# FFN tile by tile with keys as rows and squares turned through DRAM, in a fused cross-attention and FFN kernel

## The reference

```python
x = x + xattn(layernorm(x), ctx)      # 8 heads of 128; softmax of stretched scores over all 154 context rows
n = layernorm(x)
prev = n shifted down by one row within its batch (zeros first)
xr = mu_r * n + (1 - mu_r) * prev
xk = mu_k * n + (1 - mu_k) * prev
x = x + sigmoid(xr @ W_r.T) * (square(relu(xk @ W_k.T)) @ W_v.T)
```

## Time and profile before

| what | value |
|---|---|
| median of 3 runs | 744.74 us (743.87 to 744.83) |
| the profiled execution's own time | 744.54 us |
| its span in the trace | 742.7 us |
| PE busy | 736.4 us (99%) |
| DVE busy | 516.0 us (69%) |
| ACT busy | 426.8 us (57%) |
| POOL busy | 123.7 us (17%) |
| PE clock granted | full speed in all 40 slices |
| DMA | 106.52 MB, 143 GB/s |

### The profile page before, as it was taken

How to read it: one execution, slowest core, us unless ns; L and a number is a source line. 1 busy time by engine, 2 the same in 40 slices (tenths; PEclk the granted TensorE clock), 3 DMA queues, 4 the chain that set the end, 5 groups by cost and what they waited for, 6 DMA issues and landing times.

```text
span 742.7 us, 13556 instructions
## 1 busy us (share of the span) xinstructions
PE 736.4 (99%) x3948; PEld 643.0 (87%) x3948; DVE 516.0 (69%) x1085; ACT 426.8 (57%) x1204; POOL 123.7 (17%) x279
## 2 busy tenths in 40 slices
PE   9999999999999999999999999999999999999998
PEld 8957888888988888898888889888888988888887
DVE  3678987777667766666776766677666667766662
ACT  3568865575746556564655656465665646565332
POOL 1111111202121120212112021211202121120211
PEclk9999999999999999999999999999999999999999
DMA  9966643545444353545435354543535454343301
GB/s 330 252 152 172 202 136 115 148 147 177 140 146 147 117 164 87 176 142 167 129 109 159 93 175 144 163 126 115 167 84 175 143 167 128 109 156 93 112 28 43
DMA packets 87239, 106.52 MB, mean 143 GB/s; under 512 B 9999, under 2 KB 64169, under 8 KB 87211
## 3 DMA queue, kind: packets, MB, share of 16 engines
q1 hardware_dynamic: 87172, 106.15, 47.6%
q10 hardware_dynamic: 39, 0.04, 0.0%
HBM read 58.70 MB, written 47.45 MB: 143 GB/s over the span
## 4 chain that ended last, share of the span: by engine, by line
PE 90%; SPq 5%; DVE 1%; DMA 1%; ACT 1%; issue 1%; POOL 0%; POOLq 0%; DVEq 0%
PE ffn L494 12%; PE ffn L496 12%; PE ffn L495 12%; PE scores L495 9%; PE scores L496 9%; PE scores L494 9%; PE attended L496 9%; PE attended L495 9%; PE attended L494 9%; SPq L353 3%; SPq L336 1%; PE attended L544 1%; PE attended L543 1%; DMA x_rows<-normed 1%; SPq L333 1%
## 5 line engine op out<-in xcount | busy, mean ns | idle before, releaser
L494 PE MATMUL scores<-A_hi,xT_hi 128*128 128x462 f32 x372 | 129.9, 349 | 0.8 <-DVE B_lo L973 0.8
L495 PE MATMUL scores<-A_lo,xT_hi 128*128 128x462 f32 x372 | 130.4, 351 | 0.0
L496 PE MATMUL scores<-A_hi,xT_lo 128*128 128x462 f32 x372 | 130.0, 349 | 0.0
L775 ACT ACTIVATE probs<-scores,neg_max 128x154 f32<-128x154 f32 x248 | 93.2, 387 | 46.7 <-DVE neg_max L1033 46.6
L496 PE MATMUL attended<-B_hi,pT_lo 128*128 128x512 f32 x288 | 112.5, 391 | 0.0
L495 PE MATMUL attended<-B_lo,pT_hi 128*128 128x512 f32 x288 | 112.4, 390 | 0.0
L494 PE MATMUL attended<-B_hi,pT_hi 128*128 128x512 f32 x288 | 112.1, 389 | 0.0
L1033 DVE TENSOR_REDUCE neg_max<-scores 128x3 f32<-128x462 f32 (+1 forms) x93 | 53.3, 581 | 80.9 <-PE scores L496 80.9
L1334 POOL TENSOR_SCALAR var<-stats 128x1 f32<-128x1 f32 x64 | 13.2, 206 | 462.4 <-DVE stats L979 461.3
L494 PEld LDWEIGHTS scores<-A_hi,xT_hi 128*128 128x128 f32 x372 | 70.2, 189 | 8.0 <-issue 1.7
L495 PEld LDWEIGHTS scores<-A_lo,xT_hi 128*128 128x128 f32 x372 | 70.1, 188 | 5.6
(11 more groups left out here) (171 smaller groups left out, 1583.3 us busy)
## 6 DMA issues: line engine op xcount, KB each, us to landing
prob_rows<-probs SPq DMA_DIRECT2D x32, 704.0 KB, 4.1
probs_handed<-prob_rows SPq DMA_DIRECT2D x128, 176.0 KB, 3.4
x_rows<-normed SPq DMA_DIRECT2D x61, 256.0 KB, 2.4
handed<-x_rows SPq DMA_DIRECT2D x244, 64.0 KB, 1.9
x_in<-in_x SPq DMA_DIRECT2D x32, 256.0 KB, 3.0
out<-x SPq DMA_DIRECT2D x31, 256.0 KB, 3.7
wq<-in_L_xattn_Wq SPq DMA_DIRECT2D x2, 1024.0 KB, 10.6
wout<-in_L_xattn_Wout SPq DMA_DIRECT2D x1, 2048.0 KB, 20.1
```

Source lines behind the costliest of these rows:

```text
L494: te.matmul(psum, left[0], right[0], start=first, stop=False)
L495: te.matmul(psum, left[0], right[1], start=False, stop=False)
L496: return te.matmul(psum, left[1], right[0], start=False, stop=last)
L775: last = nc.scalar.activation(probs[:, q, cols], score_banks(t)[b][:, (h - h0) * J:(h - h0 + 1) * J], ACT.Exp, bias=neg_max[:, h:h + 1], a ...
```

## The change

1. Keys are made tile by tile and as rows. `key_rows(t)` holds the tile's mixed rows as the weights and streams 512 columns of W_k: 12 matmuls of 512 columns, as gates and values have. In step t TensorE now does `scores(t + 2)`, `attend(t)`, `key_rows(t - 1)`, `gate_rows(t - 1)`, `value_rows(t - 2)`, in every step. Pairs are gone; the mixed buffers and xn2T hold one tile.
2. The squares now stand as rows, so they take the way through DRAM: one store (`store_squares`), four reads (`hand_squares`), one transpose (`squares_turn`) for each tile; the last tile's are turned by TensorE (`turn_last_squares`).
3. `keep_halo` runs for each tile, and its second copy waits also for `mix("r", t)`.
4. x and x2 are read back into buffers of their own (`handed`, `handed2`), so `hand_x` no longer waits for x2's turn, nor `hand_x2` for x's.
5. `hand_probs(t + 1)` stands in step t, a step later than before, ahead of `store_probs(t + 2)`.
6. `add_x(t)` stands ahead of `x_turn(t + 3)`.
7. The raw W_v is loaded over wq's place, after wq has been turned; W_k's high part waits for W_v's turn.
8. Start and end are written out anew. At the end `value_rows(28)` moves behind `attend(31)`.

```diff
+            def key_rows(t):
+                if begun(t - 1):
+                    te.wait_ge(relu_ready, t)
+                else:
+                    te.wait_ge(W_ready, DC)
+                te.wait_ge(mixed_split["k"], t + 1)
+                ffn_rows(T[1], (mixed_hi["k"], mixed_lo["k"]), WT["k"]).then_inc(k_done, 1)
...
+            def value_rows(t):
+                if begun(t - 1):
+                    te.wait_ge(gated, t)
+                else:
                     te.wait_ge(W_ready, 3 * DC)
+                te.wait_ge(act_split, t + 1)
+                ffn_rows(T[2], (act_hi, act_lo), WT["v"]).then_inc(kv_done, 1)
...
TensorE, step:
+                if is_last(t):
+                    value_rows(t - 3)
+                key_rows(t - 1)
+                gate_rows(t - 1, turn_last_x2 if is_last(t) else None)
+                if is_last(t - 1):
+                    turn_last_squares()
+                if not is_last(t + 1):
+                    value_rows(t - 2)
+                if is_last(t - 1):
+                    last_value_rows()
TensorE, start, after attend(1):
+            scores(4); attend(2); key_rows(0); gate_rows(0)
+            scores(5); key_rows(1); gate_rows(1)
+            attend(3); value_rows(0); key_rows(2); gate_rows(2); value_rows(1)
...
ScalarE, step:
+                    exponentials(t + 2, 0)
+                mixed_high("k", t - 1)
+                    exponentials(t + 2, 1)
+                    squares_hi(t - 2)
+                mixed_high("r", t - 1)
+                    exponentials(t + 2, 2); normalise_early(t + 2); pack_hi(t + 2)
                 x_hi(t + 3)
                 x2_norm(t, s)
+                squares(t - 1)
                 probs_hi(t + 1, 0..2)
+                open_gate(t - 1, (s + 1) % 2)
ScalarE, start, after pack_hi(4):
+            squares(0); x2_norm(2); mixed_high("k", 1); probs_hi(3); open_gate(0, 0)
+            x_norm(6, 2); mixed_high("r", 1); exponentials(5, 0..1); squares_hi(0); ...
...
VectorE, step:
+                x_statistics(t + 3); open_values(t - 3); maxima(t + 2, 0)
+                x2_turn(t - 1); mix_change(t - 1); mix("k", t - 1); maxima(t + 2, 1)
+                squares_turn(t - 2); mix("r", t - 1); maxima(t + 2, 2); inverse_early(t + 2)
+                mixed_low("k", t - 1); squares_lo(t - 2); mixed_low("r", t - 1)
+                normalise_late(t + 2); pack_lo(t + 2); add_x(t)
+                x_turn(t + 3); probs_turn(t + 1); x_lo(t + 3); probs_lo(t + 1, 0..2)
VectorE, start, after mixed_low("r", 0):
+            inverse_early(4); x_turn(5); normalise_late(4); x_lo(5); x2_turn(1); pack_lo(4)
+            mix_change(1); add_x(2); probs_turn(3); mix("k", 1); x_statistics(6); probs_lo(3)
+            mixed_low("k", 1); mix("r", 1); maxima(5, 0); mixed_low("r", 1); ...
+            squares_turn(1); add_x(3); squares_lo(1); probs_turn(4); open_values(0); ...
...
GpSimd, start:
+            keep_halo(0); x2_root(2); keep_halo(1); x_root(6); keep_halo(2); x2_root(3); output(0)
def keep_halo(t, pick):
                 pool.wait_ge(halo_kept, t + 1)
+                pool.wait_ge(mixed_ready["r"], t + 1)
...
SyncE, step:
+                store_x(t + 3); store(t - 3); hand_x(t + 3); hand_probs(t + 1); store_probs(t + 2)
+                load_x(t + 4); store_x2(t); store_squares(t - 1); hand_x2(t); hand_squares(t - 1)
```

More of the change, by code:

```diff
@@ L476, in _ @@
             load_x(4, 0)
+            hand_x(5)
             store_probs(3)
@@ L481, in _ @@
             hand_probs(3)
-            hand_x(5)
+            load_x(6, 2)
+            store_squares(0)
+            store_x2(2)
+            hand_squares(0)
+            hand_x2(2)
+            store_probs(4)
+            store_x(6)
+            hand_x(6)
+            hand_probs(4)
+            store_squares(1)
+            hand_squares(1)
+            store_probs(5)
+            load_x(7, 3)
+            store_x2(3)
+            store(0, 0)
+            hand_x2(3)
+            store_squares(2)
+            hand_squares(2)
             turns(sp, step)
-            store(PAIRS - 1, 0, 2)
+            store(TILES - 2, 2)
             store_last()
@@ L732, in _ @@
             attend(1)
+            scores(4)
+            attend(2)
+            key_rows(0)
+            gate_rows(0)
+            scores(5)
+            key_rows(1)
+            gate_rows(1)
+            attend(3)
+            value_rows(0)
+            key_rows(2)
+            gate_rows(2)
+            value_rows(1)
             turns(te, step)
@@ L951, in _ @@
             for w in "kr":
[L952 removed]
+                mixed_high(w, 0)
             for b in range(3):
                 exponentials(4, b)
[L955 removed]
             normalise_early(4)
             x_hi(5)
[L958 to L959 removed]
             pack_hi(4)
+            squares(0)
             x2_norm(2, 2)
+            mixed_high("k", 1)
             for i in range(3):
                 probs_hi(3, i)
[L964 to L965 removed]
+            open_gate(0, 0)
+            x_norm(6, 2)
+            mixed_high("r", 1)
+            for b in range(2):
+                exponentials(5, b)
+            squares_hi(0)
+            exponentials(5, 2)
+            normalise_early(5)
+            squares(1)
+            mixed_high("k", 2)
+            pack_hi(5)
+            x_hi(6)
+            open_gate(1, 1)
+            mixed_high("r", 2)
+            squares_hi(1)
+            x2_norm(3, 3)
+            for i in range(3):
+                probs_hi(4, i)
+            squares(2)
+            open_gate(2, 0)
+            turns(act_e, step)
         @block.vector
@@ L1178, in step @@
+                if not ends:
+                    open_values(t - 3, (s + 1) % 2)
                 if is_tile(t + 2):
-                    for b in range(3):
-                        maxima(t + 2, b)
-                    inverse_early(t + 2)
-                if is_tile(t - 1):
-                    x2_turn(t - 1, 1 - half, pair)
-                    mix_change(t - 1, 1 - half, pair)
-                    for w in "kr":
-                        mix(w, t - 1, 1 - half, pair)
+                    maxima(t + 2, 0)
@@ new lines, in step @@
+                x2_turn(t - 1)
+                mix_change(t - 1)
+                mix("k", t - 1)
+                if ends:
+                    mixed_low("k", t - 1)
+                if is_last(t):
+                    add_x(t, g, s)
+                if is_tile(t + 2):
+                    maxima(t + 2, 1)
+                if not ends:
+                    squares_turn(t - 2)
+                mix("r", t - 1)
+                if is_tile(t + 2):
+                    maxima(t + 2, 2)
+                    inverse_early(t + 2)
@@ L1418, in _ @@
             x2_root(1)
+            keep_halo(0, 1)
+            x2_root(2)
+            keep_halo(1, 1)
+            x_root(6)
+            keep_halo(2, 1)
+            x2_root(3)
+            output(0, 0, 0)
             turns(pool, step)
```

449 lines of the change are left out of this document (219 added, 230 removed).

## The result

The changed kernel takes 742.85 us (median of 21 runs, 741.67 to 745.0); in the same sessions the kernel before took 743.97 (21 runs, 742.97 to 745.71). The ratio is 0.9986, with a 95% interval of 0.9979 to 0.9992. It is faster by 1.1 us, 0.14%: inside the 0.2% that the prediction called "same", but with an interval that leaves out no change, and with the other sign than the forecast of +1.3 us. The profiled execution took 744.13 us, 0.41 less than that of before.

A forecast was written before the change was run, and what follows sets the result against it. The prediction took TensorE's matmul distances to bound the kernel. Its terms, -4.7 + 2.0 + 1.15 + 2.2 + 0.85 + 0.15 - 0.3 = +1.3 us on 744.54, gave 745.8 us, range 741.9 to 749.0.

The forecast's parts named there:

- the matmuls: Key matmuls as 512-column rows save 5.12 us over 32 tiles; four transposes add 0.41; sum -4.7 us.
- gate_rows(1): Start: TensorE waits 2.0 us (bounds 1.3 and 2.7), through GpSimd's halo copy and root, then x_norm(6) on ScalarE.
- value_rows(1): Start: it waits 1.15 us (0 to 2.5) for open_values(0), behind squares_turn(1) and other work on VectorE.
- attend(31): End: waits 2.2 us (1.1 if add_x(30) starts at once), with squares(29) ahead of probs_hi(31) on ScalarE.
- turn_last_squares: End: waits 0.85 us (0 to 2), since ScalarE has squares_hi(30) ahead of squares(31).
- the term of 0.15 for the keys at the end: End: +0.15 us in the sum; key_rows(29) just in time (0.1), tile 31's keys within 0.1 of TensorE's work.
- the gap at the x2 transposes: End: the 0.3 us wait before the x2 transposes goes away, since they now stand inside gate_rows(30).
- The steady step: Loop: a step becomes 21.48 us and stays full; slack 1.4 us at x2_turn and 3.7 at key_rows.
- rival 3: Loop: x2 landing more than 5.1 us later than counted makes key_rows wait each step, 26 us per us; chance 0.03.
- The start: Start: nothing TensorE needs changes up to attend(2); then waits of 2.0 us at gate_rows(1) and 1.15 at value_rows(1).
- the slower rival: Start: waits compound around x_root(6) behind keep_halo(1), from 0.4 us above the sum to 749.0 us; chance 0.33.
- the faster one: Start and end: the four waits fall to lower bounds (1.3, 0, 1.1, 0), giving 741.9 us; chance 0.24.

The follow-up runs named there:

- the run with halves: Changed kernel with key_rows in 24 matmuls of 256 columns instead of 12 of 512: 748.71 us, ratio 1.0055 to the kernel before.
- the two swaps: Changed kernel with SyncE reading squares ahead of x2 each step: 769.13 us with add_x behind x_turn, 751.99 us with add_x as in the change.
- the run in which they were 2 us later: Changed kernel with SyncE's read of x2 of tile 0 waiting again for x's turn of tile 4: 743.24 us, ratio 0.9988.
- the version at 740.25 us: Changed kernel with the root and end moves, open_values(0) ahead of probs_turn(4), and squares_lo(28) behind probs_turn(31): 740.25 us, ratio 0.9946.
- the root ahead of the copy: Changed kernel with GpSimd's x_root(6) ahead of keep_halo(1) at the start: 742.54 us, ratio 0.9982 to the kernel before.

## Why the prediction was wrong in sign

The forecast was +1.3 us against the profiled execution of before; the profiled execution after is at -0.4. Term by term, measured less forecast: the matmuls +0.2, `gate_rows(1)` -1.16, `value_rows(1)` -0.82, `attend(31)` -0.24, `turn_last_squares` -0.85, the term of 0.15 for the keys at the end +0.07, the gap at the x2 transposes -0.2, the lower clock +1.55, and 0.3 less that no term had. The terms of the start are the largest error, and they alone turn the sign.

The rows for the start and for the last squares (ScalarE, VectorE, ScalarE):

```profile
94.41 0.39 ACT L809 ACTIVATE probs<-scores,neg_max 128x154 f32<-128x154 f32 x1
...
120.19 0.63 ACT L859 ACTIVATE act<-act 128x512 f32<-128x512 f32 x1
```

```profile
99.89 0.69 DVE L1027 TENSOR_TENSOR xT_lo<-xT,xT_hi 128x512 fp32r<-128x512 f32 x1 [1.70 <-ACT xT_hi L799]
...
109.35 1.13 DVE L1148 SCALAR_TENSOR_TENSOR xr<-delta,mu_r_cols,xn2T 128x128 f32<-128x128 f32 x4
```

```profile
732.24 0.63 ACT L859 ACTIVATE normed<-act 128x512 f32<-128x512 f32 x1
```

- **The matmuls: right.** -4.85 where 5.12 was forecast; -4.5 with the four transposes, against -4.7. The Trainium skill (TensorE: Matmul & The Clock Gate, "Back-to-back issue gap") gives N / 2.4 + 2.5 ns for an isolated matmul at full clock, by which an estimate for these sizes is 215.8 and 109.2 ns; the traces show 227 and 120. The measurement decides: the run with halves costs about 5 us and not the 1.0 of that estimate.
- **The steady step: right in its outcome.** 21.48 us, no wait. The slack was misjudged, though (rival 3): 5.1 us before TensorE would notice, where VectorE has only 3.2 us idle in a step, and the two swaps show that these just bear x2's delay with the addition early and don't with it late. It did not touch the sum.
- **The start: this is the step that failed.** The two terms of +2.0 and +1.15 measured +0.84 and +0.33. The mechanism was right, and the piece after `mix("r", 1)` was too: 115.7 - 111.8 = 3.9 us forecast, 114.37 - 110.48 = 3.9 measured (the root took 1.3, its lower bound). What was mis-sized is the point from which it counts. I let the exponentials of tile 4 start 0.7 us later than before, for the store of the probabilities ahead of them; they started at 94.41, before the 94.78 of the earlier trace rows, straight behind a cast, and `x_lo(5)` at 99.89 and not 101.0. So `mix("r", 1)` ended at 110.48 (109.35 + 1.13) and not 111.8, and 1.3 us less wait follows, less 0.2 since TensorE itself came earlier. The wait of 0.84 lies under the lower bound of 1.3 that the prediction gave: the bounds were for the root alone and had nothing for the point from which it counts. (The pieces listed from 101.0 on, with 0.6 for `x_lo(5)`, add up to 112.0; the slip of 0.2 does not matter.) That the transfers ahead were not what set it is shown by the run in which they were 2 us later. For `value_rows(1)` the way through DRAM was priced rightly (ready at 120.82, turned from 127.11, 6.3 us, for 122.9 to 129.0, 6.1), but the squares were ready 2.1 us ahead of the 122.9 that I gave. 1.65 of this is the same error once more: the exponentials of tile 5, which stand before them on ScalarE, started at 113.40, straight behind the cast of `xr`, which the sum has ending at 115.7 - 0.65 = 115.05. The store of the probabilities of tile 4, which the slower rival lets hold them back, had gone at 110.08.
- **attend(31): right.** 1.96 for 2.2. Not forecast: the clock behind it, 1.55 us in that execution; five of 21 executions of the change have a granted clock that low. The 0.15 of the sum for the keys of tiles 29 and 31 measured 0.22, all of it at `key_rows(31)`.
- **turn_last_squares: mis-sized.** 0.85 forecast, none measured. The way through DRAM was right (stored at 724.62, turned from 730.34, 5.7 us); the last squares ended at 732.87, and TensorE came to them at 732.98, 17.1 us after `attend(31)`, 0.3 later than my sum, while the chain was 0.5 shorter. A difference of two nearly equal times was taken for a cost.
- **The slower rival** did not come, but its mechanism exists: with one buffer for both reads `key_rows(1)`, `gate_rows(1)` and `value_rows(1)` lost 6.0 us together, and the clock another 1.6. Of the faster one, "the four waits fall to their lower bounds", half happened, for the reason it named, that VectorE ran about 1 us ahead of my count: `gate_rows(1)` fell below its bound and `turn_last_squares` to it, `value_rows(1)` came to 0.33, while `attend(31)` stayed where the sum had it. That the time lies inside the stated range is in part luck: the clock's 1.55 us, which no term had, offset the error of the start. Its chance of 0.24 was too low against 0.33 for the slower: I had let every store hold back the engine that reuses its buffer, so the errors could hardly fall on the slow side.

## What to carry to other kernels

When one edit saves a fixed amount and several small waits give it back, price each wait as a difference of two times and write down the error of each time; three waits of 0.85 to 2 us, each at the end of a chain counted 0.5 to 2 us late, turned a gain of 1 us into a forecast loss. Where an engine's in-order list goes through a store and a read and back, look for the ring, and take its spare time once, not at each station. A wait of TensorE near 2 us can be followed by a loss as large as itself, and removing it may only bring the next chain to light: order both ends together, as the version at 740.25 us did.

## What the runs showed of the hardware that I had not expected

- After some waits TensorE's granted clock fell for a stretch to the 1.2 GHz level, matmuls of 512 columns standing 427 ns apart: eight of them after an idle time of 1.8 us (the change, and the root ahead of the copy; 1.6 us lost), eight after 2.9 (one buffer), twelve after 4.1 (squares read first, with either place of the addition). Idle times of 1.6 to 1.8 us were followed by no fall in the profiles of five other versions, and none was seen behind 1.4 us or less. What decides between executions stays open.
- The slow stretch need not begin at the first matmul after the wait: in the change six stand at the usual distance first (707.54 to 708.77), with the root first it begins at the second, with x2 read last at the first.
- 25 late reads, for which VectorE waited 3.4 us each, cost TensorE under 1 us in all in one order of VectorE's list; 24 of 3.5 cost it 0.6 us a step in another.
